# Causal value products two sets later and in two halves, on one core of Trainium2

## Chip, cores and metric

The kernel runs on one core of a Trainium2 chip. The metric is the device time of one execution in microseconds (us). The kernel before took 2382.55 us (median of three runs, 2377.95 to 2383.61).

## The reference, cut to what matters

Two blocks work on x of 4 batches x 1024 tokens x 256 features: first causal attention with 16 heads of 16 features, then a two-layer network with local attention. The change touches the causal attention alone:

```python
q, k, v = proj(wq, bq), proj(wk, bk), proj(wv, bv)       # 16 heads of 16 features
scores = jnp.einsum('bhqd,bhkd->bhqk', q, k) * scale
mask = jnp.triu(jnp.full((t, t), NEG, jnp.float32), k=1)
attn = jax.nn.softmax(scores + mask, axis=-1)
out = jnp.einsum('bhqk,bhkd->bhqd', attn, v)
```

## The kernel before

`prepare` (L93) projects q, k and v, `causal_attention` (L435) makes the attention, `project_causal` (L831) the output projection, and `layers` (L1058) the rest. The change lies in `causal_attention` alone.

Causal attention works on 16 **groups**, each the four heads (HG = 4) of one quarter of a batch's heads. A group has 12 **sets** (L399 and before: SETS, NS = 12). A set is one tile of 128 keys (kt) against one chunk c of 512 queries: sets 0 to 3 are chunk 0 (kt 0 to 3), sets 4 to 11 are chunk 1 (kt 0 to 7). Keys of a later tile see only later queries, so the sets have 512, 384, 256, 128, then five times 512, 384, 256 and 128 query columns (`first_query`, L399). The four diagonal sets of each chunk (0 to 3 and 8 to 11) need the causal mask.

Each set has four steps, one per head, counted i = 0 to 47 over the group. Every engine runs its own list written out by hand, in order, and waits on semaphores:

- **TensorE (PE)**. `shifted_score` (L609, matmul L616): transposed scores of step i, keys on the partitions, into one of three PSUM banks st_ps; it waits until ScalarE has done the exponential of step i - 3. Between the steps stand **pieces** (`score_piece`, L594, matmul L598): the scores of the *next* group, queries on the partitions, from which the row maxima are taken. A group has 48 of them, 128 to 512 columns wide, in three PSUM banks s_ps, each waiting for the reduction of the piece three before it. 32 of the 48 lie on the diagonal and have a 128-column mask matmul (L601) behind them. How many pieces stand behind each step is in PIECES_AT (`beside`, L413): set 0 has 7, sets 1 to 3 have 4, 3 and 2, sets 4 to 9 have 5, 6, 6, 6, 6 and 3, sets 10 and 11 none. `shift_rows` (L604, matmul L606) turns the two halves of the maxima, behind the pieces of steps 24 and 42.
- `add_values` (L620, matmul L630): the value product of a whole set. Each of the four heads takes a 128x32 tile of the array (tile_position), in FP32, which is eight instructions on PE; the result is added up over the sets of a chunk in one bank o_ps. It stands behind the last step of a set and takes the set before it: behind step 4n + 3 come the values of set n - 1. The first one of a chunk (kt = 0) waits until ScalarE has copied the last chunk out of o_ps (o_copied).
- `turn_output` (L635, L638): four transposes of the copied output into ot_ps, for the previous group's chunk 1 behind step 11, for this group's chunk 0 behind step 31.
- **ScalarE (ACT)**: `exponential` (L695, L701), one per step, into probs, which holds three sets; the first step of set n waits for the values of set n - 3 (pv_done). `copy_output` (L703, L706) copies o_ps, for the previous group's chunk 1 ahead of exponential 5, for chunk 0 ahead of exponential 21. `copy_shift` (L691, L693) follows exponentials 24 and 42.
- **VectorE (DVE)**: `reduce_piece` (L741, L744), one per piece, `join` (L749) behind the 24th and the 48th, and `normalise` (L764, L767 and L770) behind the pieces of steps 11 and 31.
- **GpSimd (POOL)**: masks a diagonal set once its four exponentials are done (L819); its values wait for that.
- **SyncE (SP)**: `store` of the normalised output (L526), `load` of the stacks of the group three ahead (L520), `spread_shift` (L531), in this order behind one another on its queue.

Two further pieces of work share the stage: ACT and POOL split the network's weights in two of the 16 groups (`high_parts`, `low_parts`). The last group has no following one, so no pieces.

Of the kernel before, what the change touches and what calls it, by code (L numbers as in the profile page):

```python
# [25 lines left out]
CH = 512  # L26
NC = T // CH
TC = CH // P
# [406 lines left out]
def causal_attention(nc, x_all, stacks, ident, ident_b, causal_b, passed, a):  # L435
# [6 lines left out]
    with ExitStack() as ctx:  # L442
# [144 lines left out]
        def _(pe):  # L587
# [32 lines left out]
            def add_values(group, n):  # L620
                r, slot = group
                c, kt = SETS[n]
                q0 = first_query(c, kt)
                pe.wait_ge(exp_done.sem, when(exp_done, group, NS * HG, n * HG + HG - 1))
                if n in DIAGONAL:
                    pe.wait_ge(masked.sem, when(masked, group, len(DIAGONAL), DIAGONAL.index(n)))
                if kt == 0:
                    pe.wait_ge(o_copied.sem, when(o_copied, group, NC, c - 1))
                for h in range(HG):
                    mm = pe.matmul(o_ps[h * VW:(h + 1) * VW, q0:CH], v_sb[:, slot, kt, h * VW:(h + 1) * VW],  # L630
                                   probs[:, n % 3, h, q0:CH], start=kt == 0, stop=kt == (c + 1) * TC - 1,
                                   tile_position=(0, h * VW))
                mm.then_inc(pv_done.sem, 1)
# [16 lines left out]
            def group_work(group, previous, following):  # L650
# [3 lines left out]
                for i in range(NS * HG):  # L654
                    n = i // HG
                    shifted_score(group, i)
                    if following:
                        for _ in range(PIECES_AT[i]):
                            score_piece(following, piece)
                            piece += 1  # L660
                        if i in SHIFT_AT:

                            pe.wait_ge(att_ready.sem, when(att_ready, group, NC, SHIFT_AT[i] - 1))
                            shift_rows(following, SHIFT_AT[i])
                    if i % HG == HG - 1:
                        if n >= 1:
                            add_values(group, n - 1)
                        elif previous:
                            add_values(previous, NS - 1)
                        if n == 2 and previous:  # L670
                            pe.wait_ge(shift_copied.sem, when(shift_copied, group, 2, 1))
                            turn_output(previous, 1)
                        if n == 7:
# [5 lines left out]
                if not following:  # L679
                    add_values(group, NS - 1)  # L680
# [6 lines left out]
        def _(act):  # L687
# [32 lines left out]
            def group_work(group, previous, following):  # L720
                for i in range(NS * HG):
                    if i == HG + 1 and previous:
                        copy_output(previous, 1)
                    if i == 5 * HG + 1:
# [12 lines left out]
        def _(dve):  # L737
# [40 lines left out]
            def group_work(group, previous, following):  # L778
                piece = 0
                for i in range(NS * HG):  # L780
# [4 lines left out]
                    if i == 2 * HG + HG - 1 and previous:  # L785
                        normalise(previous, 1)
                    if i == 7 * HG + HG - 1:
# [1261 lines left out]
```

## Time and profile before

| | |
|---|---|
| median of three runs | 2382.55 us |
| profiled execution, its own time | 2368.78 us |
| its span in the trace | 2367.0 us |
| PE busy | 2082.5 us, 88% |
| DVE busy | 1404.6 us, 59% |
| ACT busy | 1223.0 us, 52% |
| POOL busy | 827.1 us, 35% |
| mean granted TensorE clock | 0.963 |

A busy time of PE is that of modelled, pipelined matmuls: a record goes on after the next matmul has begun. So the distance from one start to the next says what a matmul costs, and its own duration what must pass until its result is there.

### The profile page before, as it was taken

The numbers are of one execution on the slowest core, as the hardware profiler recorded it, in microseconds if no ns is written. First come the engines' busy times: TensorE is split into PE (matmuls) and PEld (weight loads), VectorE is DVE, ScalarE is ACT, GpSimd is POOL, SyncE is SP. The second block draws the span as 40 slices with busy tenths as digits, with TensorE's granted clock in tenths as the row PEclk, the third lists the DMA queues.
The fourth block names the chain that finished last, engine by engine and source line by source line (L and its number), as shares of the span: only waits on it lengthen the run. The fifth ranks groups of instructions, "written<-read, shape, count | busy, mean of one in ns | idle before, by whom it ended". The sixth has DMA issues, their size and how long they took to land.

```text
span 2367.0 us, 35438 instructions
## 1 busy us (share of the span) xinstructions
PE 2082.5 (88%) x11968; PEld 1203.6 (51%) x11968; DVE 1404.6 (59%) x3354; ACT 1223.0 (52%) x2904; POOL 827.1 (35%) x711
## 2 busy tenths in 40 slices
PE   5577899999988738999999989989989989989988
PEld 3332333333332514665665665665566566566556
DVE  5467777778773526546646646645645745645744
ACT  1121666666666315735735735644653753754663
POOL 2233212111231336326425425515514613614620
PEclk9896999999999978999999999999999999999999
DMA  4646853455520631000000000102000010010000
GB/s 144 156 133 132 176 76 64 65 82 81 103 96 13 180 111 77 19 27 10 19 27 10 19 27 10 48 23 99 28 18 27 10 37 19 19 37 18 19 1 27
DMA packets 130689, 135.21 MB, mean 57 GB/s; under 512 B 50556, under 2 KB 107472, under 8 KB 129488
## 3 DMA queue, kind: packets, MB, share of 16 engines
q1 hardware_dynamic: 129936, 124.05, 22.2%
q0 software_dynamic: 576, 8.91, 1.0%
q8 instruction: 98, 1.61, 0.3%
q14 instruction: 79, 0.65, 0.1%
HBM read 81.80 MB, written 50.86 MB: 56 GB/s over the span
## 4 chain that ended last, share of the span: by engine, by line
PE 45%; ACT 7%; DVE 6%; issue 4%; POOL 2%; DMA 0%; SPq 0%; DVEq 0%; ACTq 0%; POOLq 0%
PE qkv_ps L1297 12%; PE s_ps L1337 5%; PE qkv_ps L1350 5%; PE pt_ps L1403 3%; PE s_ps L1390 3%; PE s_ps L1471 3%; PE o_ps L1428 3%; ACT p_sb L1565 2%; PE turn_ps L1322 2%; PE pt_ps L1390 2%; PE pt_ps L1471 2%; PE o_ps L1471 2%; PE o_ps L1390 2%; POOL inv_norm L1702 1%; PE turn_ps L1412 1%
## 5 line engine op out<-in xcount | busy, mean ns | idle before, releaser
L744 DVE TENSOR_REDUCE piece_negmax<-s_ps 128x1 f32<-128x512 f32 (+3 forms) x768 | 372.9, 550 | 94.1 <-PE s_ps L601 91.9
L701 ACT ACTIVATE probs<-st_ps 128x512 f32<-128x512 f32 (+3 forms) x768 | 330.1, 495 | 181.7 <-PE st_ps L616 179.4
L1297 PE MATMUL qkv_ps<-w_qkv,x_in 128*128 128x512 f32 x768 | 363.4, 607 | 24.3 <-SPq L1236 17.3
L1565 ACT ACTIVATE p_sb<-p_sb,negmax 128x256 f32<-128x256 f32 (+1 forms) x512 | 249.4, 490 | 49.2 <-DVE negmax L1803 49.0
L598 PE MATMUL s_ps<-k_stack,q_stack 96*128 96x512 bf16 (+3 forms) x768 | 249.0, 345 | 28.1 <-DVEq L739 12.0
L616 PE MATMUL st_ps<-q_stack,k_stack 98*128 98x512 bf16 (+3 forms) x768 | 232.9, 333 | 16.3 <-ACT probs L701 14.3
L1803 DVE CUSTOM_DVE_ANT_0 p_sb<-s_ps,band 128x256 f32<-128x256 f32 (+1 forms) x512 | 185.3, 401 | 94.0 <-PE s_ps L1337 92.1
L1581 ACT COPY p_t<-pt_ps 128x512 f32<-128x512 f32 (+1 forms) x256 | 143.4, 560 | 182.8 <-PE pt_ps L1403 181.4
L819 POOL TENSOR_SCALAR_AFFINE_SELECT probs<-probs 128x512 f32<-128x512 f32 x128 | 81.2, 635 | 430.5 <-ACT probs L701 430.5
L1710 POOL TENSOR_TENSOR rot_c<-qn,turn_by 128x512 f32<-128x512 f32 x128 | 174.6, 1384 | 141.5 <-PE turn_ps L1322 113.1
L1297 PEld LDWEIGHTS qkv_ps<-w_qkv,x_in 128*128 128x128 f32 x768 | 137.6, 194 | 152.3 <-issue 138.6
L1794 DVE TENSOR_TENSOR rot_s<-qn,turn_by 128x256 f32<-128x256 f32 x256 | 200.5, 842 | 0.3
L1702 POOL TENSOR_TENSOR inv_norm<-sum_sq,neg_half 128x16 f32<-128x16 f32 x64 | 187.5, 2930 | 5.3
L1403 PE MATMUL pt_ps<-ident,p_sb 128*128 128x128 f32 x960 | 161.6, 288 | 26.8 <-ACT p_t L1581 26.8
L1715 POOL TENSOR_TENSOR rot_c<-rot_c,rot_s 128x1024 f32<-128x1024 f32 x64 | 155.2, 2425 | 60.2 <-DVE rot_s L1794 60.2
L1774 DVE TENSOR_REDUCE sum_sq<-squares 128x16 f32<-128x1024 f32 x64 | 77.9, 1217 | 160.2 <-ACT squares L1544 160.2
L630 PE MATMUL o_ps<-probs,v_sb 128*32 128x512 f32 (+3 forms) x1536 | 164.4, 500 | 1.1 <-POOL probs L819 0.7
L616 PEld LDWEIGHTS st_ps<-q_stack,k_stack 98*128 98x128 bf16 x768 | 69.0, 98 | 156.1 <-ACT probs L701 114.5
L1337 PE MATMUL s_ps<-k_t,q_t 64*128 64x256 f32 (+1 forms) x1024 | 139.0, 390 | 10.4 <-DVE negmax L1803 9.5
L1403 PEld LDWEIGHTS pt_ps<-ident,p_sb 128*128 128x128 f32 x960 | 101.5, 141 | 91.4 <-issue 84.6
L1390 PE MATMUL s_ps<-hn_t,w_ffn 128*128 128x512 f32 (+1 forms) x528 | 143.9, 424 | 0.0
L1720 POOL TENSOR_SCALAR var_eps<-mean_var 128x4 f32<-128x4 f32 x16 | 5.4, 336 | 390.0 <-DVE mean_var L1826 390.0
(142 smaller groups left out, 3505.8 us busy)
## 6 DMA issues: line engine op xcount, KB each, us to landing
qk_scratch<-parts SPq DMA_DIRECT2D x64, 192.0 KB, 2.8
q_stack<-qk_scratch SPq DMA_DIRECT2D x96, 128.0 KB, 6.5
k_stack<-qk_scratch SPq DMA_DIRECT2D x96, 128.0 KB, 7.1
w_ffn<-ffn_weights POOLq DMA_DIRECT2D x4, 2176.0 KB, 11.5
v_scratch<-v_out SPq DMA_DIRECT2D x32, 256.0 KB, 2.6
v_sb<-v_scratch SPq DMA_DIRECT2D x16, 512.0 KB, 10.3
x_in<-xt_scratch SPq DMA_DIRECT2D x16, 512.0 KB, 3.7
turn_by<-in_rotary SPq DMA_DIRECT2D x8, 1024.0 KB, 5.5
```

Source lines behind the costliest of these rows:

```text
L598: mm = pe.matmul(s_ps[i % 3][:, 0:kw], q_stack[0:STK, slot, h, qt * P:(qt + 1) * P], k_stack[0:STK, slot, h, k0:k0 + kw], start=True, stop ...
L616: pe.matmul(st_ps[i % 3][:, q0:CH], k_stack[0:STK + SHIFT, slot, h, kt * P:(kt + 1) * P], q_stack[0:STK + SHIFT, slot, h, c * CH + q0:(c + ...
L701: act.activation(probs[:, n % 3, h, q0:CH], st_ps[i % 3][:, q0:CH], ACT.Exp).then_inc(exp_done.sem, 1)
L744: dve.tensor_reduce(piece_negmax[:, h, i % NP:i % NP + 1], s_ps[i % 3][:, 0:kw], AX.X, ALU.max, negate=True).then_inc(piece_done.sem, 1)
L1297: mm = pe.matmul(qkv_ps[:, part * CH:(part + 1) * CH], x_in[:, k, w * P:(w + 1) * P], w_qkv[:, k, part * INNER:(part + 1) * INNER], start= ...
L1337: mm = pe.matmul(s_ps[side][:, (h + 1) * PW - ((w + 1) * P - k0):(h + 1) * PW], q_t[r, w % 2, p, :], k_t[r, p, k0:(w + 1) * P], start=True ...
L1390: mm = pe.matmul(up_pair(c, j)[bank][0:rows, :], w_up(w, k, tile)[:, 0:rows], hn_t[:, h, k, :], start=n == 0, stop=n == len(steps) - 1)
L1403: mm = pe.transpose(pt_ps[:, (h * 2 + kt) * P:(h * 2 + kt + 1) * P], p_sb[:, u % 4, h, kt * P:(kt + 1) * P], ident[:, :])
L1565: act.activation(p_sb[:, u % 4, h, k0:PW], p_sb[:, u % 4, h, k0:PW], ACT.Exp, scale=-1.0, bias=negmax[:, u % 4, h:h + 1], accum_out=total[ ...
L1702: pool.tensor_tensor(inv_norm[:, :], sum_sq[:, 1, :], neg_half[:, 0:2 * H2], ALU.pow)\
L1794: dve.tensor_tensor(dst[:, :, o], src[:, :, i], turn_by[:, w, 2 * j + 1, o].unsqueeze(1) .to_broadcast([P, H2, half]), ALU.mult).then_inc( ...
L1803: dve.tensor_tensor_reduce(p_sb[:, u % 4, h, k0:PW], s_ps[u % 2][:, h * PW + k0:(h + 1) * PW], band[:, k0:PW], 1.0, BIG, ALU.add, ALU.min, ...
```

## The change

`add_values` takes a half. For a set with 0 < kt < last, the columns are cut in the middle: half 0 is issued behind the second step of a set, half 1 behind its fourth. The first and the last set of a chunk stay whole and go with half 0. The values issued during set n are those of set n - 2. ACT's copies of the output move four steps later (to ahead of exponentials 9 and 25), PE's turns to behind steps 15 and 35, and DVE's normalisation with them. Behind the very last step the values of sets 10 and 11 remain.

```diff
-            def add_values(group, n):
+            def add_values(group, n, half):
+
                 r, slot = group
                 c, kt = SETS[n]
                 q0 = first_query(c, kt)
-                pe.wait_ge(exp_done.sem, when(exp_done, group, NS * HG, n * HG + HG - 1))
-                if n in DIAGONAL:
-                    pe.wait_ge(masked.sem, when(masked, group, len(DIAGONAL), DIAGONAL.index(n)))
-                if kt == 0:
-                    pe.wait_ge(o_copied.sem, when(o_copied, group, NC, c - 1))
+                mid = (q0 + CH) // 2 if 0 < kt < (c + 1) * TC - 1 else CH
+                lo, hi = ((q0, mid), (mid, CH))[half]
+                if lo == hi:
+                    return
+                if half == 0:
+                    pe.wait_ge(exp_done.sem, when(exp_done, group, NS * HG, n * HG + HG - 1))
+                    if n in DIAGONAL:
+                        pe.wait_ge(masked.sem, when(masked, group, len(DIAGONAL), DIAGONAL.index(n)))
+                    if kt == 0:
+                        pe.wait_ge(o_copied.sem, when(o_copied, group, NC, c - 1))
                 for h in range(HG):
-                    mm = pe.matmul(o_ps[h * VW:(h + 1) * VW, q0:CH], v_sb[:, slot, kt, h * VW:(h + 1) * VW],
-                                   probs[:, n % 3, h, q0:CH], start=kt == 0, stop=kt == (c + 1) * TC - 1,
+                    mm = pe.matmul(o_ps[h * VW:(h + 1) * VW, lo:hi], v_sb[:, slot, kt, h * VW:(h + 1) * VW],
+                                   probs[:, n % 3, h, lo:hi], start=kt == 0, stop=kt == (c + 1) * TC - 1,
                                    tile_position=(0, h * VW))
-                mm.then_inc(pv_done.sem, 1)
+                if hi == CH:
+                    mm.then_inc(pv_done.sem, 1)
...
+                    if i % 2:
+                        if n >= 2:
+                            add_values(group, n - 2, i % HG // 2)
+                        elif previous:
+                            add_values(previous, NS - 2 + n, i % HG // 2)
                     if i % HG == HG - 1:
-                        if n >= 1:
-                            add_values(group, n - 1)
-                        elif previous:
-                            add_values(previous, NS - 1)
-                        if n == 2 and previous:
+                        if n == 3 and previous:
                             pe.wait_ge(shift_copied.sem, when(shift_copied, group, 2, 1))
                             turn_output(previous, 1)
-                        if n == 7:
+                        if n == 8:
...
                 if not following:
-                    add_values(group, NS - 1)
+                    for n in (NS - 2, NS - 1):
+                        for half in range(2):
+                            add_values(group, n, half)
                     pe.wait_ge(att_ready.sem, when(att_ready, group, NC, 0))
                     turn_output(group, 1)
...
-                    if i == HG + 1 and previous:
+                    if i == 2 * HG + 1 and previous:
                         copy_output(previous, 1)
-                    if i == 5 * HG + 1:
+                    if i == 6 * HG + 1:
                         copy_output(group, 0)
...
-                    if i == 2 * HG + HG - 1 and previous:
+                    if i == 3 * HG + HG - 1 and previous:
                         normalise(previous, 1)
-                    if i == 7 * HG + HG - 1:
+                    if i == 8 * HG + HG - 1:
                         normalise(group, 0)
```

## Rows read from the trace of the kernel before

**Rows 1.** Page, part 1: busy us, share of the span, instructions.
```profile
PE 2082.5 (88%) x11968; PEld 1203.6 (51%) x11968; DVE 1404.6 (59%) x3354; ACT 1223.0 (52%) x2904; POOL 827.1 (35%) x711
```
**Rows 2.** Line L616: all its score matmuls, ns minimum/median/maximum, first and last start.
```profile
L616 PE MATMUL st_ps<-q_stack,k_stack x768: 216/376/635, 223.5 to 761.6; 98*128 98x512 bf16 x96, 98*128 98x384 bf16 x32, 98*128 98x256 bf16 x32, 98*128 98x128 bf16 x32
```
**Rows 3.** Windows: us; busy PE, PEld, DVE, ACT, POOL; clock, DMA share, GB/s.
```profile
326.00:360.00 34.00, 32.41 (x242) 13.09 (x245) 26.51 (x62) 22.53 (x55) 6.46 (x10) 1.00 0.48 71
...
734.00:768.00 34.00, 25.18 (x185) 7.79 (x184) 2.04 (x6) 22.55 (x57) 7.72 (x12) 0.99 0.06 13
```
**Rows 4.** Page, part 5: reductions of the pieces, and value products.
```profile
L744 DVE TENSOR_REDUCE piece_negmax<-s_ps 128x1 f32<-128x512 f32 (+3 forms) x768 | 372.9, 550 | 94.1 <-PE s_ps L601 91.9
...
L630 PE MATMUL o_ps<-probs,v_sb 128*32 128x512 f32 (+3 forms) x1536 | 164.4, 500 | 1.1 <-POOL probs L819 0.7
```
**Rows 5.** Timeline of PE in one group: its first step, and one of 256 columns.
```profile
397.49 0.39 PE L616 MATMUL st_ps<-q_stack,k_stack 98*128 98x512 bf16 x1
...
403.05 0.28 PE L616 MATMUL st_ps<-q_stack,k_stack 98*128 98x256 bf16 x1
```
**Rows 6.** Timeline of PE: set 7 and the turn behind it.
```profile
416.73 0.39 PE L616 MATMUL st_ps<-q_stack,k_stack 98*128 98x512 bf16 x1
416.95 0.33 PE L598 MATMUL s_ps<-k_stack,q_stack 96*128 96x384 bf16 x1
417.12 0.22 PE L601 MATMUL s_ps<-causal_b,ident_b 128*128 128x128 bf16 x1
417.18 0.38 PE L616 MATMUL st_ps<-q_stack,k_stack 98*128 98x512 bf16 x1
...
419.19 0.34 PE L598 MATMUL s_ps<-k_stack,q_stack 96*128 96x384 bf16 x1 [0.26 <-DVE piece_negmax L744]
419.36 0.22 PE L601 MATMUL s_ps<-causal_b,ident_b 128*128 128x128 bf16 x1
419.51 1.07 PE L630 MATMUL o_ps<-probs,v_sb 128*32 128x512 f32 x8
420.51 0.66 PE L638 MATMUL ot_ps<-ident,o_sb 128*128 128x128 f32 x4
421.00 0.38 PE L616 MATMUL st_ps<-q_stack,k_stack 98*128 98x512 bf16 x1
```
**Rows 7.** Timeline of PE: the group's last blocks of values, and the next group's first step.
```profile
428.57 0.85 PE L630 MATMUL o_ps<-probs,v_sb 128*32 128x384 f32 x8
429.36 0.34 PE L616 MATMUL st_ps<-q_stack,k_stack 98*128 98x128 bf16 x3
...
430.17 0.64 PE L630 MATMUL o_ps<-probs,v_sb 128*32 128x256 f32 x8
430.75 0.39 PE L616 MATMUL st_ps<-q_stack,k_stack 98*128 98x512 bf16 x1
```
**Rows 8.** Timeline of DVE in the same group: reductions in sets 3 to 7.
```profile
406.36 5.42 DVE L744 TENSOR_REDUCE piece_negmax<-s_ps 128x1 f32<-128x384 f32 x10
...
417.38 2.80 DVE L744 TENSOR_REDUCE piece_negmax<-s_ps 128x1 f32<-128x384 f32 x6 [0.50 <-PE s_ps L601]
```
**Rows 9.** Timeline of ACT: exponentials, a copy of the output, a copy of the shifts.
```profile
403.43 1.26 ACT L701 ACTIVATE probs<-st_ps 128x256 f32<-128x256 f32 x4 [0.41 <-PE st_ps L616]
...
410.36 0.58 ACT L706 COPY o_sb<-o_ps 128x512 f32<-128x512 f32 x1
410.82 1.61 ACT L701 ACTIVATE probs<-st_ps 128x512 f32<-128x512 f32 x3
...
414.24 0.25 ACT L693 CAST shift_sb<-ot_ps 32x128 bf16<-32x128 f32 x1
```
**Rows 10.** Timeline of PE: the first half's shifts, then steps 25 and 26.
```profile
413.98 0.23 PE L606 MATMUL ot_ps<-ident_b,negmax_parts 128*32 128x128 bf16 x1
414.14 0.39 PE L616 MATMUL st_ps<-q_stack,k_stack 98*128 98x512 bf16 x1
...
414.48 0.38 PE L616 MATMUL st_ps<-q_stack,k_stack 98*128 98x512 bf16 x1
```

## Prediction

> **What bounds the kernel now.** The page's first part makes TensorE the busiest engine, 2082.5 us of the span [rows 1], but only one stage is touched: the score matmuls of line L616 run from 223.5 to 761.6 us [rows 2], 16 groups in some 540 us. The windows over that stage come next. In a steady one of 34 us PE shows 32.4 us, DVE 26.5, ACT 22.5 and POOL 6.5, at a granted clock of 1.00; in the last group, which has no pieces, DVE has 2.0 and PE 25.2 [rows 3]. The steady window is PE's, with DVE not far behind, and the 32.4 flatters PE, since its records run on past the next start.
>
> So I went to PE's timeline for one group and took distances between starts. The group begins at 397.49 [rows 5] and the next one at 430.75 [rows 7]: a **period of 33.26 us**. A 512-column score takes 0.22 us of it, a mask 0.06 (416.73 to 416.95, 417.12 to 417.18) [rows 6]. A whole block of values over 512 columns takes 1.00 (419.51 to 420.51) [rows 6], over 384 0.79 and over 256 0.58 [rows 7]. The slope is 0.21 us per 128 columns, so 0.14 is left at width zero. Before the block there is a gap too: the mask ahead of 419.51 starts at 419.36 and streams its 128 columns in 0.053, so about 0.10 passes idle [rows 6]. **A block of values costs 0.24 us plus 1.67 ns per column**, and the 0.24 is paid once per block, whatever its width.
>
> What PE must do in a group, by these prices: scores are 18432 columns, or 36 times 0.22, 7.9 us; pieces as many, 7.9; 32 masks of 0.06, 1.9; values 4608 column positions at 1.67 ns, 7.7, and 12 blocks at 0.24, 2.9; two turns at 0.49, 1.0 (420.51 to 421.00) [rows 6]; two shifts at 0.16, 0.3 [rows 10]. Sum 29.6. The other **3.6 us are waits**, for a free bank: a piece waits for the reduction three before (0.26 at 419.19) [rows 6], a score for the exponential three before. They come from lumps: while a block of 1.00 us runs, DVE and ACT empty their three banks (DVE idle 0.50 before 417.38 [rows 8], right behind the block of set 6), and PE afterwards finds them behind. DVE works 5.42 us without a gap over ten reductions [rows 8].
>
> **The change, part by part.** *Splitting.* Eight of twelve sets have 0 < kt < last (1 and 2, 5 to 10), so 8 blocks more per group: 8 times 0.24 is **+1.9 us** of PE. The columns stay the same. PE's floor becomes 31.5. It is the edit whose price I am surest of, because three widths give the same 0.14.
>
> By the Trainium skill ("TensorE: Matmul & The Clock Gate", the section that asks why 56 ns and not 53.3) a matmul carries only about 2.5 ns beyond its columns; eight instructions more would then cost 0.02 us per block and the floor would hardly move, some 0.2 us per group where the rows give 1.9. The rows disagree with it at every width. Another page, "TensorEngine Tiling (Array Packing)", Key Properties, says that a change of tiling mode drains the engine, and its rule fits the idle 0.10 ahead of each block of 128x32 tiles.
>
> *Two sets of delay.* The exponentials and the masks of a set are long done when its values come. Of this little is to be had: the value products waited 0.7 us for POOL in the whole execution [rows 4]. The third buffer of probs is handed back just ahead of the score that needs it, on PE's own order (the second half of set n - 3 stands ahead of set n's first score), so ACT gets no new wait from pv_done.
>
> *The copies of the output.* This is a wait that the change brings. The values of a chunk's first set need ACT's copy. Before, they stood behind step 7 (and 23) and the copy ahead of exponential 5 (and 21), two exponentials ahead of what PE had already asked for. Now values and copy both sit at step 9 (and 25): PE issues score 9, then needs a copy that stands behind exponential 8, one step back. Queued behind that wait on PE are all further scores and pieces, and ACT and DVE wait for those.
>
> Step 9: score 8 starts at S; its exponential can start at S + 0.38 (403.05 [rows 5] to 403.43 [rows 9]), and with the 384-wide ones ahead (some 0.43 each, between the 0.31 and 0.54 of the rows) arriving as fast as ACT does them I take 0.16 more; then 0.31 for it and 0.58 for the copy [rows 9], 0.09 to reach PE: S + 1.5. PE is ready at S + 0.6 (two 256-wide scores 0.22, a masked piece 0.28, the gap 0.10). **+0.9 us**; bounds 0.7 (ACT not behind) and 1.2.
>
> Step 25: PE turns the shifts at U, ACT casts them at U + 0.26 for 0.25 (413.98 and 414.24) and only then copies, 0.58 [rows 9, 10], plus 0.09: U + 1.18. PE is ready at U + 0.6 (step 26 would start at U + 0.50 [rows 10], plus the gap). **+0.6 us**; bounds 0.3 (PE late for other reasons) and 0.8. In that set two pieces stand behind step 24 and DVE's join runs just then, with no block of values between to cover it: 0.4 more, part of the walk below.
>
> *What the halves give back.* I walked the group with the starts and durations above, step by step: PE in order, each score 0.09 us behind the end of the exponential three before, each piece likewise behind its reduction, reductions at 0.21 to 0.61 us by width (ten of mixed width in 5.42). Against the times of the trace:
> Sets 0 and 1: 5.56 before (397.49 to 403.05 [rows 5]), 5.06 after: the values are those of sets 10 and 11, three blocks of 128 columns in place of 128 and 512.
> Sets 2 to 6: 13.68 (to 416.73 [rows 6]), 15.24 after: four short or whole sets of values and a split more (+0.5), the two copy waits (+1.5), the join (+0.4), less some 0.8 of waits in sets 4 and 5 that go.
> Set 7: 4.27 (to 421.00 [rows 6]), 3.99 after: the turn of 0.49 has left, a split of 0.24 has come.
> Sets 8 to 10: 8.36 (to 429.36 [rows 7]), 8.58 after: values of 6, 7 and 8 in halves, 4.0 us, in place of 7, 8, 9 whole, 3.1; the turn +0.49; 1.2 of waits gone, DVE is fed throughout.
> Set 11: 1.39 (to 430.75 [rows 7]), 1.39 after.
> Sum 34.26, or **+1.0 us per group**: +1.9 for the blocks, +1.5 for the copies, -2.4 of the 3.6 us of waits. Of the old waits 1.2 remain, because in sets 7 to 9 PE is then full without a gap.
>
> *The rest.* The turns and normalisations only move (same instructions, DVE has them between reductions). On SP, the store of the previous group's chunk 1 goes out some 2.4 us later, and behind it the 13 loads and then the shifts of the first half; the loads are for three groups later, the shifts are used some 16 us on, so nothing waits: zero, and up to 0.3 us per group were that cover gone. The last group has no pieces; its ACT works 22.5 of 34 us and PE is not full [rows 3], halves may save some 0.2 us in a few sets, the two copies and the extra blocks behind the last step take as much: zero, within 1 us.
>
> **Sum.** 15 groups at +1.0 is +15 us. The profiled execution (2368.78 us, span 2367.0) would become 2384; it lies 13.8 below the median of the runs shown, and against that median of 2382.55 I forecast **2397.5 us**, 0.6% slower. What can be told from no change is about 0.3%, 7 us, or 0.5 us per group.
>
> **Rivals.**
> *Same.* The copy waits cost little: if PE comes to steps 9 and 25 late anyway, held by DVE's banks, 1.0 of the 1.5 us is no addition. Then +0 per group, 2383. For it: DVE is 26.5 of 34 us busy [rows 3]. Against: at step 9 few pieces are out (set 2 has three), and at 25 the chain runs through ACT from the shifts themselves. 0.21.
> *Faster.* The second block is nearly free, its 0.24 falling into time in which PE would wait for a bank. That is the skill page's 2.5 ns read as a mechanism of this kernel, and also what the splitting would have to do. Where DVE is the bound (sets 4 to 6) it holds; were it so in sets 7 to 10 too, 1.0 of the 1.9 us goes, and with the copy waits halved the group takes 34.26 - 1.0 - 0.8 = 32.5, or -0.8: 2371. It decides once the waits left, old and new, sum to less than 1.7 us per group, since 31.5 + 1.7 is today's period. Against: the gap and the offset stand at each block in the rows. 0.14.
> *Worse than forecast.* The copy waits at their upper bounds (2.0) and DVE starved behind them so that the halves give back 1.7 only: +2.2 per group, 2415. 0.10.
> *The change does nothing that it says* (values wait as before): excluded, the order on PE is written out; a loss by SP's queue is in the bounds.
> The forecast itself has 0.55.
>
> **Numbers.** Slower by over 0.3%: 0.55 + 0.10 = 0.65; within 0.3%: 0.21; faster: 0.14. The range leaves out the far faster case and the end of the worse one: 2378 to 2414. The forecast's own part is 2391 to 2407.
>
> **What would show it.** The period of a group in PE's timeline 34.3 us. L630 with 2048 matmuls, and 0.14 beside the columns in each half (a 256-column half from start to start 0.57). Waits of PE's value products on ACT's copy (L706), 0.9 and 0.6 us in each group, some 23 us in all, where the trace now shows nearly none. DVE's idle time in sets 7 to 9 under 0.3 us per set, ACT's likewise less; one gap of over 1 us on DVE in set 6. Wrong would be: a period under 33.3, or halves that cost less than 0.1 beside their columns, or values that begin right behind scores 9 and 25.

## The result, and the profile after

The changed kernel takes 2404.38 us (median of four runs, 2402.21 to 2407.03), the kernel before 2380.45 (four runs): a ratio of 1.010, interval 1.0081 to 1.012, some 24 us slower. The forecast was 15 us slower. The profiled executions lie 33 us apart (2402.21 against 2368.78), because that of before is a low one: 30 runs of before, taken beside the first experiments, go from 2371.3 to 2384.7. Up to some 10 us of the gap between the two traces is therefore no effect of the change; a part of it can be pointed to below.

The page after, its first part, the reductions and the value products (the columns of [rows 1] and [rows 4]):

```profile
PE 2108.5 (88%) x12992; PEld 1226.2 (51%) x12992; DVE 1414.8 (59%) x3354; ACT 1237.0 (52%) x2904; POOL 826.9 (34%) x711
...
L754 DVE TENSOR_REDUCE piece_negmax<-s_ps 128x1 f32<-128x512 f32 (+3 forms) x768 | 380.5, 550 | 131.9 <-PE s_ps L601 103.3
...
L636 PE MATMUL o_ps<-probs,v_sb 128*32 128x256 f32 (+3 forms) x2560 | 194.2, 376 | 19.1 <-POOL probs L829 11.4
```

Against [rows 1, 4] the value products are 2560 instructions in place of 1536, busy 194.2 us in place of 164.4, and stand idle 19.1 us in place of 1.1. (The prediction's 2048 is a wrong sum: 8 more blocks of 8 instructions in 16 groups are 1024 more.)

A steady window after (columns of [rows 3]):

```profile
360.00:394.00 34.00, 32.01 (x298) 14.03 (x298) 26.29 (x60) 22.64 (x52) 6.45 (x10) 1.00 0.45 70
```

It looks like that of [rows 3]: PE 32.0, DVE 26.3, ACT 22.6 of 34 us. A loss of 4% in the stage does not show in it: the busy time of PE includes the new blocks and the tails of modelled matmuls. The period shows it. In the timeline of ACT the copy of the previous group's output recurs once in a group, at step 9:

```profile
346.67 0.58 ACT L716 COPY o_sb<-o_ps 128x512 f32<-128x512 f32 x1
...
381.29 0.58 ACT L716 COPY o_sb<-o_ps 128x512 f32<-128x512 f32 x1
...
415.91 0.58 ACT L716 COPY o_sb<-o_ps 128x512 f32<-128x512 f32 x1
```

**34.62 us**, where [rows 5, 7] gave 33.26; the forecast was 34.3. And the two places at which the forecast put the new wait, in PE's timeline of one group, steps 8 to 10 and the shifts to step 26:

```profile
415.26 0.27 PE L616 MATMUL st_ps<-q_stack,k_stack 98*128 98x256 bf16 x1
...
415.65 0.27 PE L616 MATMUL st_ps<-q_stack,k_stack 98*128 98x256 bf16 x1
416.64 1.06 PE L636 MATMUL o_ps<-probs,v_sb 128*32 128x512 f32 x8 [0.71 <-POOL probs L829]
417.63 0.28 PE L616 MATMUL st_ps<-q_stack,k_stack 98*128 98x256 bf16 x1
...
427.23 0.23 PE L606 MATMUL ot_ps<-ident_b,negmax_parts 128*32 128x128 bf16 x1
427.39 0.39 PE L616 MATMUL st_ps<-q_stack,k_stack 98*128 98x512 bf16 x1
...
427.68 0.22 PE L601 MATMUL s_ps<-causal_b,ident_b 128*128 128x128 bf16 x1
428.37 1.06 PE L636 MATMUL o_ps<-probs,v_sb 128*32 128x512 f32 x8 [0.48 <-ACT o_sb L716]
429.37 0.39 PE L616 MATMUL st_ps<-q_stack,k_stack 98*128 98x512 bf16 x1
```

Behind score 9 PE could begin at 415.65 + 0.11 + 0.10 = 415.86 and begins at 416.64, 0.78 us later; behind the mask of step 25 it could at 427.83 and begins at 428.37, 0.54 later. What POOL and ACT did meanwhile:

```profile
413.53 0.63 POOL L829 TENSOR_SCALAR_AFFINE_SELECT probs<-probs 128x512 f32<-128x512 f32 x1 [2.53 <-ACT probs L711]
415.89 0.63 POOL L829 TENSOR_SCALAR_AFFINE_SELECT probs<-probs 128x512 f32<-128x512 f32 x1 [1.73 <-ACT probs L711]
...
427.50 0.25 ACT L703 CAST shift_sb<-ot_ps 32x128 bf16<-32x128 f32 x1 [0.51 <-PE ot_ps L606]
427.66 0.57 ACT L716 COPY o_sb<-o_ps 128x512 f32<-128x512 f32 x1
```

The first wait is put down to POOL, and that is not so. POOL's operation at 415.89 masks set 1; the values at 416.64 are those of set 0, whose mask was done at 414.16. It ends at 416.52, the copy at 415.91 + 0.58 = 416.49: the profile names the one that ended later, and only the code says which of them PE waits for. The second wait is the chain of the forecast: shifts on PE, cast, copy, values.

DVE in the same group:

```profile
410.71 4.21 DVE L754 TENSOR_REDUCE piece_negmax<-s_ps 128x1 f32<-128x128 f32 x9 [2.98 <-PE s_ps L601]
...
426.24 2.47 DVE L754 TENSOR_REDUCE piece_negmax<-s_ps 128x1 f32<-128x128 f32 x6
430.02 4.52 DVE L754 TENSOR_REDUCE piece_negmax<-s_ps 128x1 f32<-128x512 f32 x9 [1.31 <-PE s_ps L598]
435.15 1.29 DVE L754 TENSOR_REDUCE piece_negmax<-s_ps 128x1 f32<-128x512 f32 x2 [0.61 <-PE s_ps L601]
```

Where PE stands at step 25, DVE runs dry for 1.31 us. Behind that it works 4.52 us without a gap, where before it had 2.80 us behind a gap of 0.50 [rows 8].

The end of the second half of the maxima, on PE, DVE and POOL (the join is L763 to L771; behind it PE turns the shifts):

```profile
441.98 0.28 PE L616 MATMUL st_ps<-q_stack,k_stack 98*128 98x256 bf16 x1
442.50 0.22 PE L606 MATMUL ot_ps<-ident_b,negmax_parts 128*32 128x128 bf16 x1 [0.24 <-DVE negmax_parts L771]
...
441.34 0.53 DVE L763 COPY negmax<-piece_negmax 128x8 f32<-128x8 f32 x1
442.18 0.17 DVE L771 TENSOR_TENSOR negmax_parts<-negmax,negmax_parts 128x16 bf16<-128x16 f32 x1
...
441.21 0.64 POOL L829 TENSOR_SCALAR_AFFINE_SELECT probs<-probs 128x512 f32<-128x512 f32 x1 [2.79 <-ACT probs L711]
```

PE could send the shifts at 441.98 + 0.11 = 442.09 and sends them at 442.50, 0.41 us later. The first copy of the join takes 0.53 us; in the middle of the group it takes 0.17. It ends at 441.87, 0.02 behind POOL's mask of set 8.

### The profile page after: what moved, and what is told of

It reads as the page before. It is cut to its first block, busy times and chain, and to the rows that moved or that the text cites. A ratio compares the mean times of both kernels' runs of the same rounds, so it can differ in the third digit from the quotient of the medians.

```text
span 2400.5 us, 37486 instructions
## 1 busy us (share of the span) xinstructions
PE 2108.5 (88%) x12992; PEld 1226.2 (51%) x12992; DVE 1414.8 (59%) x3354; ACT 1237.0 (52%) x2904; POOL 826.9 (34%) x711
## 4 chain that ended last, share of the span: by engine, by line
PE 45%; ACT 7%; DVE 6%; issue 4%; POOL 2%; DMA 0%; SPq 0%; DVEq 0%; ACTq 0%; POOLq 0%
PE qkv_ps L1307 12%; PE s_ps L1347 5%; PE qkv_ps L1360 5%; PE pt_ps L1413 3%; PE s_ps L1400 3%; PE s_ps L1481 3%; PE o_ps L1438 3%; ACT p_sb L1575 2%; PE turn_ps L1332 2%; PE pt_ps L1400 2%; PE pt_ps L1481 2%; PE o_ps L1481 2%; PE o_ps L1400 2%; POOL inv_norm L1712 1%; PE turn_ps L1422 1%
## 5 line engine op out<-in xcount | busy, mean ns | idle before, releaser
L754 DVE TENSOR_REDUCE piece_negmax<-s_ps 128x1 f32<-128x512 f32 (+3 forms) x768 | 380.5, 550 | 131.9 <-PE s_ps L601 103.3
L711 ACT ACTIVATE probs<-st_ps 128x512 f32<-128x512 f32 (+3 forms) x768 | 343.2, 491 | 189.0 <-PE st_ps L616 186.1
L598 PE MATMUL s_ps<-k_stack,q_stack 96*128 96x512 bf16 (+3 forms) x768 | 243.8, 347 | 26.2 <-DVE piece_negmax L754 12.6
L616 PE MATMUL st_ps<-q_stack,k_stack 98*128 98x512 bf16 (+3 forms) x768 | 244.0, 339 | 11.2 <-ACT probs L711 6.0
L636 PE MATMUL o_ps<-probs,v_sb 128*32 128x256 f32 (+3 forms) x2560 | 194.2, 376 | 19.1 <-POOL probs L829 11.4
L616 PEld LDWEIGHTS st_ps<-q_stack,k_stack 98*128 98x128 bf16 x768 | 69.7, 98 | 147.1 <-ACT probs L711 91.2
```

The lines of the kernel that those rows point to most:

```text
L598: mm = pe.matmul(s_ps[i % 3][:, 0:kw], q_stack[0:STK, slot, h, qt * P:(qt + 1) * P], k_stack[0:STK, slot, h, k0:k0 + kw], start=True, stop ...
L616: pe.matmul(st_ps[i % 3][:, q0:CH], k_stack[0:STK + SHIFT, slot, h, kt * P:(kt + 1) * P], q_stack[0:STK + SHIFT, slot, h, c * CH + q0:(c + ...
L636: mm = pe.matmul(o_ps[h * VW:(h + 1) * VW, lo:hi], v_sb[:, slot, kt, h * VW:(h + 1) * VW], probs[:, n % 3, h, lo:hi], start=kt == 0, stop= ...
L711: act.activation(probs[:, n % 3, h, q0:CH], st_ps[i % 3][:, q0:CH], ACT.Exp).then_inc(exp_done.sem, 1)
L754: dve.tensor_reduce(piece_negmax[:, h, i % NP:i % NP + 1], s_ps[i % 3][:, 0:kw], AX.X, ALU.max, negate=True).then_inc(piece_done.sem, 1)
```

## Experiments

The **period** below is the distance from group to group, from first score to first score, in each trace's steady stretch. It repeats to 0.01 us there unless said otherwise. The time of a whole execution does not: the runs of one kernel spread by some 10 us. The ratio is against runs of the kernel before on the same chip.

| kernel | period, us | ratio, interval |
|---|---|---|
| before | 33.25 | |
| changed | 34.62 | 1.010 (1.0081 to 1.012) |
| changed, early copies | 33.41 | 1.0021 (1.001 to 1.0032) |
| changed, whole blocks | 33.64 | 1.0027 (1.0016 to 1.0038) |
| before, adjacent halves | 33.29 | 1.0007 (0.9995 to 1.0018) |
| before, late copies | 33.98 | 1.0044 (1.0024 to 1.0064) |
| before, second half two steps later | 33.39 | 1.0002 (0.9989 to 1.0016) |
| before, pairs | 33.48 | 1.002 (1.0011 to 1.003) |
| pairs and three halves | 33.52 | 1.0015 (1.0005 to 1.0026) |
| pairs, sets 8 and 9 later | 34.4 to 36.6 | 1.0132 (1.01 to 1.0164) |
| changed, early copies, factor 1.12 | 33.03 | 0.9991 (0.9979 to 1.0003) |
| before, factor 1.12 | 34.48 | 1.0085 (1.0062 to 1.0107) |
| changed, early copies, factor 1.10 | 33.47 | 1.0024 (1.0014 to 1.0035) |
| changed, early copies, factor 1.14 | 34.05 | 1.0043 (1.0027 to 1.0059) |

### The copy wait taken out

```diff
-                    if i == 2 * HG + 1 and previous:
+                    if i == HG + 3 and previous:
                         copy_output(previous, 1)
-                    if i == 6 * HG + 1:
+                    if i == 5 * HG + 3:
                         copy_output(group, 0)
```

> The changed kernel with ScalarE's output copies two exponentials earlier (ahead of exponentials 7 and 23 instead of 9 and 25), so that TensorE finds the copy done at steps 9 and 25. Theory (the copy waits cost what the changed kernel's timeline shows, about 0.8 and 0.5 us per group): the wait of the value products on the copy falls to nearly 0, the period of a group falls from 34.62 to 33.3 to 33.6 us, the time to within 0.4% of the kernel before. Rival (TensorE only waits elsewhere, since DVE or the columns bound it anyway): the period stays at 34.2 us or more, the time 0.7% or more above the kernel before.

Period 33.41 us, 1.21 less than the changed kernel, and the waits of the value products on the copy are gone from the list of waits. The rival falls. The two waits read in the trace, 0.78 and 0.54, sum to 1.32; taking them away gives back 1.21, so almost none was standing in for another wait. What was left of the change costs 0.16 us a group.

### The delay without the halves

```diff
-                mid = (q0 + CH) // 2 if 0 < kt < (c + 1) * TC - 1 else CH
-                lo, hi = ((q0, mid), (mid, CH))[half]
+                lo, hi = ((CH, CH), (q0, CH))[half]
...
-                if half == 0:
+                if half == 1:
```

> The changed kernel with whole blocks: all columns of a set behind the fourth step, still two sets later; copies ahead of exponentials 9 and 25, values of a chunk's first set now behind steps 11 and 27. Theory (the delay is neutral, the loss is the eight extra blocks and the copy waits): period 33.1 to 33.5 us, same time as before within 0.3%. Rival (the delay itself costs, by the later turns and normalisations): period 33.8 us or more.

33.64 us: neither. There is no copy wait in this kernel (its values of a chunk's first set come two steps behind the copy), and it has before's twelve blocks, so **the delay alone, with the copies, turns and normalisations that move with it, costs 0.39 us a group**. DVE shows where. Sets 10 and 11 have no pieces, and DVE is idle from its last join to the next group's first piece. In the kernel before and in this one:

```profile
398.04 5.10 DVE L744 TENSOR_REDUCE piece_negmax<-s_ps 128x1 f32<-128x128 f32 x11 [3.23 <-PE s_ps L601]
```
```profile
405.87 6.44 DVE L753 TENSOR_REDUCE piece_negmax<-s_ps 128x1 f32<-128x128 f32 x14 [3.65 <-PE s_ps L601]
```

The idle time has grown by 0.42 us, as the period has by 0.39: sets 10 and 11 now hold the values of sets 8 and 9 (512 and 384 columns) in place of 9 and 10 (384 and 256). By the starts of their first scores these two sets take 2.36 and 1.60 us in place of 2.15 and 1.39, and set 10 starts at the same time in the group as before (29.68 and 29.71 us). So the whole loss lies in these two sets.

This kernel against the one with early copies is the experiment on the halves: values two sets late and no copy wait in either, 33.64 against 33.41 (the copies themselves stand two exponentials apart). **Halves gain 0.23 us a group** over whole blocks in this order, though PE has 8 visits more (a visit: PE enters the 128x32 tiles and leaves them again).

### What the 0.24 us of a block belong to

```diff
+                mid = (q0 + CH) // 2 if 0 < kt < (c + 1) * TC - 1 else CH
+                for lo, hi in ((q0, mid), (mid, CH)):
+                    if lo == hi:
+                        continue
+                    for h in range(HG):
+                        mm = pe.matmul(o_ps[h * VW:(h + 1) * VW, lo:hi], v_sb[:, slot, kt, h * VW:(h + 1) * VW],
...
```

> The kernel before with the eight sets cut into halves that are issued one right behind the other, no score between them. Theory A (a fixed cost at each block, 0.14 us behind the gap of 0.10 in front): the two blocks take 0.14 us more than one, period 33.24 plus up to 1.1. Theory B (the 0.24 us belongs to the change between 128x128 scores and 128x32 tiles, paid once per visit whatever the number of blocks): two adjacent halves of 256 take 1.00 us as one of 512 does, period 33.2 to 33.4 and the same time. By the 2.5 ns per matmul of the Trainium skill's page on TensorE also nearly the same, 0.02 us per pair.

PE's timeline in this kernel:

```profile
423.98 1.07 PE L634 MATMUL o_ps<-probs,v_sb 128*32 128x256 f32 x16
424.98 0.39 PE L616 MATMUL st_ps<-q_stack,k_stack 98*128 98x512 bf16 x1
```

Sixteen instructions take 1.00 us from start to start, as eight did [rows 6]; over all steady groups it is 1.004 against 0.998. The period is 33.29, 0.04 above before. Theory B: the price is one of **entering and leaving the 128x32 tiles**, not of a block. That the values are also FP32 and the scores bf16 does not explain it: the shifts are bf16 and stand in 128x32 tiles, and their 128 columns take 0.16 us where a mask in 128x128 takes 0.06 [rows 10, 6], with a gap of 0.10 in front (426.91 + 0.22 to 427.23 in the changed kernel).

The Trainium skill, "TensorE: Matmul & The Clock Gate" (the section that asks why 56 ns and not 53.3), gives each matmul about 2.5 ns beyond its columns, an estimate of 0.02 us for eight more; here eight more inside a visit cost 0.006. The Trainium skill, "TensorEngine Tiling (Array Packing)", Key Properties, says that changing the tiling mode drains TensorE; it gives no time, and here each visit pays 0.24 us for coming and going.

In the change each half is a visit of its own, and each pays: 0.57 us for 256 columns, 0.46 for 192, as in these rows of the changed kernel (2 x 0.57 = 1.14 against the 1.00 of one block, with the gap of 0.10 in front twice).

```profile
406.78 0.64 PE L636 MATMUL o_ps<-probs,v_sb 128*32 128x256 f32 x8
407.35 0.28 PE L616 MATMUL st_ps<-q_stack,k_stack 98*128 98x256 bf16 x1
...
409.03 0.53 PE L636 MATMUL o_ps<-probs,v_sb 128*32 128x192 f32 x8
409.49 0.28 PE L616 MATMUL st_ps<-q_stack,k_stack 98*128 98x128 bf16 x2
```

### The copy wait put into the kernel before

```diff
-                    if i == HG + 1 and previous:
+                    if i == HG + 3 and previous:
...
-                    if i == 5 * HG + 1:
+                    if i == 5 * HG + 3:
```

> The kernel before with its copies two exponentials later, ahead of exponentials 7 and 23, the steps behind which the values of a chunk's first set stand: the changed kernel's copy wait alone. Theory: waits of the value products on the copy of about 0.7 to 0.9 us at step 7 and 0.3 to 0.7 at step 23, period 34.0 to 34.8 us, time 0.5 to 0.9% above the kernel before. Rival (the wait only stands in for waits on banks): period under 33.6, time within 0.3%.

33.98 us, 0.73 more than before: a hair under the theory's 34.0 and clear of the rival. The whole time, 0.44% longer, lies between the two expectations. The step 7 wait is there:

```profile
414.87 1.06 PE L630 MATMUL o_ps<-probs,v_sb 128*32 128x512 f32 x8 [0.65 <-ACT o_sb L706]
```

At step 23 there is none: in this order the copy is ahead of exponential 23, and the shifts and their cast come only a set later. So the second half of this expectation missed. That the second wait needs step 25, behind shifts and cast, is read from the order in the code and not tested by itself. All 0.7 us appear between the starts of sets 1 and 2 (3.31 us in place of 2.59), and no later set gives any of it back.

### Halves without the delay, and fewer visits

The second half moved alone:

```diff
+                    if i % HG == 1:
+                        if n >= 2:
+                            add_values(group, n - 2, 1)
+                        elif previous:
+                            add_values(previous, NS - 2 + n, 1)
...
+                            add_values(group, n - 1, 0)
```

> The kernel before, its eight sets in halves of which only the second one is later, by two steps; first half, copies, turns and normalisations stay. It takes the halves without the delay of a set. Theory (the halves give back a little more than their 1.9 us of visits, as early copies against whole blocks with the same delay showed, 33.41 against 33.64; the delay is what costs 0.4): period 32.8 to 33.1 us, 0.1 to 0.4% faster than before. Rival (without the delay the halves only fill TensorE): 33.3 to 34.0 us.

33.39 us (one group in the stretch 33.62), no gain: the rival's lower end. The halves' 0.23 does not carry over to another schedule.

Two visits fewer:

```diff
+VALUES_AT = {1: [0], 2: [1], 4: [2, 3], 5: [4], 6: [5], 7: [6], 8: [7], 9: [8], 10: [9]}
+VALUES_LAST = [10, 11]
```

> The kernel before, with the values of sets 2 and 3, and those of 10 and 11, in one visit each (behind step 19, and behind the next group's step 3): two changes of tile shape fewer. Theory (a visit costs 0.24 us whatever it holds, and work leaves sets 10 and 11, where DVE has no pieces): set 11 takes 0.6 us less, the next set 0 0.2 to 0.5 more, period 32.7 to 33.1 us, 0.2 to 0.5% faster. Rival (the time goes to other waits): 33.2 us or more.

33.48, so this expectation fails too, though each of its parts is seen in DVE's timeline:

```profile
409.12 3.08 DVE L749 TENSOR_REDUCE piece_negmax<-s_ps 128x1 f32<-128x128 f32 x7 [2.74 <-PE s_ps L603]
412.52 2.14 DVE L749 TENSOR_REDUCE piece_negmax<-s_ps 128x1 f32<-128x256 f32 x4 [0.32 <-PE s_ps L603]
...
421.82 1.75 DVE L749 TENSOR_REDUCE piece_negmax<-s_ps 128x1 f32<-128x384 f32 x3 [0.48 <-PE s_ps L603]
```

The stretch without pieces is 0.49 us shorter (2.74 in place of 3.23), but the longer visits behind steps 3 and 19 open gaps of 0.32 and 0.48 in what had been eleven and ten reductions without one [rows 8]. PE has half a microsecond less to do and the group is 0.23 longer: **the sum of PE's work is not what sets the period**.

The same pairs, with halves in three sets:

```diff
-                mid = (q0 + CH) // 2 if 0 < kt < (c + 1) * TC - 1 else CH
+                mid = (q0 + CH) // 2 if n in (5, 6, 7) else CH
...
```

> The kernel with pairs, and halves for sets 5, 6 and 7 alone, their second half two steps later. Theory (halves pay where DVE works without a gap, in sets 6 to 8 of the program): 0.1 to 0.3 us below the period of the pairs. Rival (three more visits, 0.7 us, on a full TensorE): 0.2 us or more above it.

33.52 us (one group 33.83), 0.04 above the pairs. Neither theory: the three extra visits are hidden, and gain nothing.

The pairs again, with two wide blocks moved into sets 10 and 11:

```diff
-VALUES_AT = {1: [0], 2: [1], 4: [2, 3], 5: [4], 6: [5], 7: [6], 8: [7], 9: [8], 10: [9]}
+VALUES_AT = {1: [0], 2: [1], 4: [2, 3], 5: [4], 6: [5], 7: [6], 8: [7], 10: [8], 11: [9]}
```

> The kernel with pairs, but the values of sets 8 and 9 one set later, so that sets 10 and 11, in which DVE has no pieces, hold 512 and 384 columns of values in place of 384 and none. Theory (the delay costs because wide blocks move into the stretch without pieces and DVE starts the next group later): 0.4 to 1.2 us above the period of the pairs, and DVE's longest idle time of each group grows by as much. Rival (delay of values as such costs nothing there): within 0.2 us of it.

The groups take 34.4 to 36.6 us, irregularly, and the granted clock tells them apart. Two of the eleven steady groups (from 375.44 and from 552.95) hold no stretch of low clock; they take 34.4 us, 0.92 above the pairs. DVE's idle time ahead of the first piece is 3.65 us behind such a group, 0.91 more than the 2.74 of the pairs, and 4.95 where the clock was low in set 11:

```profile
375.98 3.08 DVE L749 TENSOR_REDUCE piece_negmax<-s_ps 128x1 f32<-128x128 f32 x7 [4.95 <-PE s_ps L603]
...
410.38 3.08 DVE L749 TENSOR_REDUCE piece_negmax<-s_ps 128x1 f32<-128x128 f32 x7 [3.65 <-PE s_ps L603]
```

So without the clock the theory's size holds too. The other nine groups have the clock at 0.50 around their start or their end: those with 1.2 to 1.5 us of it take 35.0, those with 5.3 to 5.6 us take 36.5 to 36.6. Two of the group ends in windows of 4 us (columns of [rows 3]), the first with the low clock, the second without:

```profile
368.00:372.00 4.00, 2.74 (x17) 1.09 (x19) 2.52 (x7) 3.03 (x9) 0.63 (x1) 0.97 0.00 0
372.00:376.00 4.00, 3.78 (x26) 0.98 (x19) 0.02 (x1) 1.00 (x6) 1.27 (x2) 0.61 0.03 6
```
```profile
406.00:410.00 4.00, 2.81 (x23) 0.88 (x24) 0.65 (x4) 1.72 (x7) 1.26 (x3) 1.00 0.02 4
```

Taking the block out of set 9 also lets PE reach the shifts of step 42 early, where it then waits 1.1 us for DVE, in both; so the edit is not the pure test it was meant to be, and why the clock falls in one and not in the other stays open.

### The placing of the pieces

```diff
-        upto += cols * 1.08
+        upto += cols * 1.12
```

> The changed kernel with early copies, and the pieces placed faster along the scores (factor 1.12 in place of 1.08: the last one behind step 37 in place of 39, the second half's shifts behind step 40 in place of 42). In the changed kernel set 10 took 2.35 us where the forecast had 1.95. Theory (PE waits there for DVE's join, which ends late): set 10 falls to 2.0 to 2.1 us and the period from 33.41 to 33.0 to 33.2, as long as the denser pieces cost nothing earlier. Rival (the whole group is bound by DVE plus the stretch without pieces, which only gets longer): 33.4 us or more.

> Control: the kernel before with the same factor 1.12. If the earlier join helps any schedule, its period too falls, from 33.24 to under 33.1 us (set 10 waits 0.50 us for the join there); if DVE has no time to take the pieces faster with whole blocks, it stays at 33.2 us or rises to 33.8.

The period of the changed order falls to 33.03 us (one group 33.30), 0.2 **below** the kernel before, and the same factor makes the kernel before 1.23 us longer, to 34.48, which is beyond both of its expectations. For the changed order the expected period is there, but not by the expected way. Set 10 goes from 2.35 only to 2.29. By the starts of the sets the gain is in sets 6 to 9 (13.52 us in place of 14.62), while sets 4 and 5 take 0.80 more. The kernel before, with its whole blocks, does not bear the denser pieces: it loses 0.47 us in set 2 and 0.88 in sets 4 and 5. The time of the 1.12 kernel is 0.9991 of before, interval to 1.0003: better in the period, not by a measurable amount in the whole.

> The changed kernel with early copies and factor 1.10: the halves' schedule between 1.08 (33.41 us) and 1.12 (33.03 us). If the gain comes from where single pieces fall around step 24 (one in place of two ahead of the first half's shifts), this one, with one piece behind step 24 too, is at 33.0 to 33.2 us; if it comes from the earlier end of all pieces it lies halfway, 33.2 to 33.3.

> The same with factor 1.14: last piece behind step 36, shifts behind steps 23 and 39. If the earlier end of the pieces is what gains, 32.8 to 33.0 us and a time 0.1 to 0.3% below the kernel before; if DVE has no more room and the stretch without pieces only grows, 33.2 us or more.

33.47 and 34.05 us. Factor 1.10 fails both of its readings. For 1.14 the first fails; the second has the number (33.2 us or more), and DVE's idle time ahead of the first piece has indeed grown, from 2.98 us with factor 1.08 to 4.42. The periods at 1.08, 1.10, 1.12 and 1.14 (33.41, 33.47, 33.03, 34.05) follow neither "the earlier the better" nor "one piece behind step 24". Up to step 24 the kernels of 1.10 and 1.12 start every set within 0.02 us of each other; from there that of 1.10 is first ahead (29.29 to 29.38 us at set 10) and then loses 0.5 in set 10 alone (2.82 us against 2.29). Part of that can be pointed to. In set 10 of the 1.10 kernel the cast of the join takes 0.50 us, under POOL's mask; in the 1.12 kernel the mask begins behind the join, no part of the join takes over 0.18, and its first copy, directly behind a 512-wide reduction, takes 0.17:

```profile
435.44 0.50 DVE L769 CAST negmax_parts<-negmax 128x16 bf16<-128x16 f32 x1
...
435.25 0.65 POOL L829 TENSOR_SCALAR_AFFINE_SELECT probs<-probs 128x512 f32<-128x512 f32 x1 [2.58 <-ACT probs L711]
```
```profile
434.69 0.17 DVE L763 COPY negmax<-piece_negmax 128x8 f32<-128x8 f32 x1
```

The wait for the join does not vanish with earlier pieces, because the shifts move with the last piece and PE comes to them earlier too: it waits 0.24 us at 1.08, 0.83 at 1.10, 0.18 at 1.12 and, in set 9, 0.58 at 1.14.

## Why the prediction came out as it did

*Direction and range:* right. 2404.38 lies in 2378 to 2414, and the likeliest case was the one that happened. The group was forecast at +1.0 us and is at +1.37. Most of the mechanism held, with errors both ways in its terms.

*The price of a visit, 0.24 us:* right as it applied here. A half of 256 columns takes 0.57 us from start to start, as forecast, and the experiment with adjacent halves shows that the word block was wrong: it is the change to the 128x32 tiles and back. The rival that made the second block nearly free (faster, 0.14) would have been right for two halves in one visit; a half between two scores is a visit of its own.

*The copy waits, +0.9 and +0.6:* in the trace 0.78 and 0.54, and 1.21 together when taken away. (The page gives the value products 19.1 us of idle time ahead of them where 23 were forecast, most of it under POOL's name.) The rival "same" had them largely absorbed; the early copies refute it.

*The walk through the group:* by the starts of the first scores, forecast and trace are 5.06 and 5.09 us for sets 0 and 1, 15.24 and 15.16 for sets 2 to 6, 3.99 and 4.02 for set 7, **8.58 and 8.99 for sets 8 to 10**, 1.39 and 1.36 for set 11. In sets 2 to 6 two errors cancel, which is luck: the copies cost 0.3 less than the 1.5 in it, and without them these sets take 13.95 us (early copies), 0.2 more than the walk had. The step that was mis-sized is the waits given back in sets 8 to 10 ("1.2 of waits gone, DVE is fed throughout"). One of them did not go: PE stands for the join of the second half, 0.50 us in the profile of before and still 0.24 after, which is the 0.41 us between the starts shown above. Of the 8.58, sets 8 and 9 as measured (3.93 and 2.71) leave 1.94 for set 10, and it takes 2.35. DVE was not fed throughout either: its idle time was forecast under 0.3 us in each of sets 7 to 9 and is 0.11, 0.77 and 0.45, 1.33 in all where before has 2.17. Fifteen groups of 0.4 us are 6 us.

*Why the join ends late:* **DVE's small copy stands while POOL masks.** The copy at 441.34 takes 0.53 us in place of 0.17 and ends 0.02 us behind POOL's mask of set 8 (441.21 + 0.64). In before it takes 0.35 (427.23 to 427.58) and the mask ends at 427.56. All fourteen traces agree: the four operations of the join take 0.15 to 0.18 us wherever no operation of POOL runs beside them, and each of the 236 that take over 0.2 ends 0.01 to 0.04 behind the end of one of POOL's, whichever of the four it is. The code has no wait of DVE on the mask. The reductions and the normalisation read PSUM and are not lengthened by it (a 512-wide one 0.68 to 0.69 us with a mask beside it and without). Without the 0.36 us the join would end at 441.99 and PE would wait some 0.05; that is an estimate from these rows, no run moved the mask alone. The prediction has no such term, and in the change the join begins 0.13 us into the mask, where before it began 0.31 into it.

*"Of the delay little is to be had":* it is worse, the delay costs 0.39 us (shown by whole blocks, with DVE's idle stretch as its place). The net of halves and delay was forecast at -0.5 us (+1.9 - 2.4) and is +0.16.

*Groups taken as steady that are not:* the sum used the steady group 15 times and nothing for the last. In the two groups with the weight splitting the changed kernel takes 3.98 and 3.49 us more than before (43.39 and 42.91 against 39.41 and 39.42, from copy to copy of chunk 1's output). PE there stops for ACT's four conversions; before and after, in windows of 4 us behind that stop (columns of [rows 3]):

```profile
269.00:273.00 4.00, 1.28 (x13) 0.44 (x12) 1.83 (x5) 4.00 (x5) 3.85 (x4) 0.92 0.64 130
273.00:277.00 4.00, 3.61 (x14) 1.73 (x15) 2.27 (x4) 3.46 (x7) 4.00 (x2) 0.50 1.11 120
277.00:281.00 4.00, 3.50 (x16) 0.75 (x14) 3.93 (x8) 1.20 (x2) 2.73 (x2) 0.72 1.08 115
281.00:285.00 4.00, 4.00 (x25) 1.41 (x25) 3.50 (x8) 2.60 (x6) 0.00 (x0) 1.00 1.09 263
```
```profile
275.00:279.00 4.00, 1.18 (x14) 0.47 (x13) 1.49 (x3) 4.00 (x6) 3.61 (x2) 0.96 1.01 164
279.00:283.00 4.00, 4.00 (x21) 1.67 (x20) 2.77 (x6) 2.42 (x5) 4.00 (x3) 0.50 1.09 129
283.00:287.00 4.00, 2.51 (x8) 0.69 (x7) 3.95 (x6) 1.24 (x3) 2.21 (x1) 0.50 1.10 132
287.00:291.00 4.00, 3.84 (x15) 0.94 (x15) 1.12 (x4) 1.73 (x4) 0.00 (x0) 0.50 1.03 301
291.00:295.00 4.00, 3.79 (x25) 1.57 (x23) 3.49 (x7) 2.73 (x6) 0.00 (x0) 0.84 1.05 448
```

The granted clock falls to 0.50, 1.2 GHz, in both. It is back after 6.8 us before and after 13.7 in the changed kernel, where PE's busy time in the meantime is once 2.51 of 4 us; in the second such group it is 3.4 and 13.6. The halves are not the reason: the changed kernel with whole blocks has 13.7 us of it in both groups, and takes 42.29 and 42.55 us; nor are the copy waits, with early copies it is 13.6 us, 42.03 and 42.07. What the low clock costs apart from the waits was not isolated.

The last two groups, from the first score to the last normalisation, take 66.8 us in place of 62.8, and 1.4 of that is a steady group's share. In the last one PE waits 0.9 us at step 9, and the granted clock is 0.77 and 0.50 in the 8 us behind 768, where before shows 1.00 in its last group. Here it is the copies: with early copies the two groups take 61.4 us, less than before.

These three places make 2.6, 2.1 and 2.6 us beyond the steady 1.37, forecast as zero. With 15 times 1.37 that is 28 us between the two traces, more than the 24 between the medians. The profiled before had a mean granted clock of 0.963, the 30 runs of before beside the first experiments 0.959 to 0.962, the changed kernel's four runs 0.956 to 0.958, so the usual run of before probably pays some of these 7 us too.

*What the profiled before owes to luck:* the first score of group 1 waited 0.65 us in it and 3.59 in the changed kernel, at a DMA share near 1.0 in most of the 16 us ahead of both. The profiles of the first eight experiments have 1.1 to 4.7 there, among them adjacent halves with 2.25 and late copies with 3.22, whose order up to there is that of before but for one edit, so I count it to the spread and not to the change; it was not tested. Behind the last normalisation, where the two kernels are the same, the changed one takes 2.3 us more (1603.6 against 1601.3; the other kernels 1600.0 to 1604.4). With the 28 us these two make up the 33 between the traces.

## What to carry to other kernels

When work is moved on two in-order queues, put the positions of producer and consumer side by side: a copy that had stood two exponentials ahead of what its reader had already asked for lost that lead, and 1.2 of the 1.4 us of loss per group came from this alone, not from the cut into halves. When a wait is on one engine's small operation, look at what a third engine does beside it: here a mask on POOL held DVE's copy, and with it PE. Small tiles between large ones pay for each visit and not for each instruction, so cutting inside a visit is nearly free (0.006 us for eight instructions more) and cutting across visits is not (0.24). A schedule balanced to tenths on three engines has parameters that belong together: the factor that made one order better made the other 1.2 us worse per group, so an order should not be judged with the other's parameters.

## What I had not expected of the hardware

Two adjacent blocks of 128x32 tiles cost hardly more than one: sixteen instructions 1.004 us, eight 0.998. DVE's small copies, casts and subtractions in SBUF, 0.15 to 0.18 us alone, last until POOL's operation beside them is done: 0.53 us at 441.34 under a mask, and 2.34 us for the cast in the splitting groups, under POOL's subtractions of 2.5 us. And the low clock can decide what a group takes: in the pairs with sets 8 and 9 later, with the same work in every steady group, 34.4 us without it and 36.6 with 5.6 us of it.
